# Transposing the 128-row tiles of x1 as pairs of 64-row halves, with the two waits of a tile's transposes made into one per pair

## The chip, the cores and the metric

The kernel runs on one NeuronCore of a Trainium2 chip. The time is device time in microseconds of one execution; the median of three runs is given. The engines are TensorE (PE in the profile; its weight loads are PEld), VectorE (DVE), ScalarE (ACT), GpSimd (POOL), and SyncE (SP), which here only issues DMAs.

## The reference, cut to what matters

The input x is 8 x 32 x 512 x 512 in f32 (268 MB). Two layers:

```python
x = x + conv3x3_int8(group_norm(x), weight, bias)   # layer 0; its result is called x1
x = x + irfft2(R * rfft2(group_norm(x))[low modes]) # layer 1: 32 x 16 modes, mixing channels
```

Layer 0 normalises, quantises to integers with one scale for the whole tensor, and convolves. Layer 1 needs only 16 frequencies along the width and 32 along the height, so its forward transform is made as small matrix products.

## The kernel before, in words

Three stages follow each other.

1. Statistics of x: 128 groups of 2 MB are read and summed (up to about 660 us).
2. The middle stage (about 660 to 2290 us), which the change touches. It works on 256 tiles `t`, 32 for each of the 8 images. A tile is 32 channels x 16 image rows x 512 columns, 1 MB, laid out as 128 partitions (4 rows x 32 channels) by 4 groups `g` of 512. A ring `ring` of XS = 9 slots holds the tiles.
3. The mixing of modes (about 2290 to 2330 us) and then the inverse transform, added to x1 and stored (to the end).

In the middle stage one loop over `i` is written out on every engine, and each engine runs its instructions in the written order:

- SP loads tile t with four DMAs of 256 KB (L242). It may load into a slot once the tile that was there has been stored, transposed and squared.
- ACT scales one half of tile i+1 (`scaled`, L337); DVE scales the other half and makes the quantised image and a shifted copy (L557 to L575).
- PE convolves tile i-2: 48 bf16 matmuls of 32 weight columns and 512 moving columns (`conv`, L732), four of them side by side in four column strips of the array.
- DVE adds the convolution to x in the slot, in two halves (`combine`, L580): the slot now holds x1. GpSimd stores it with four DMAs (L296).
- PE transposes tile i-4 (`turn_x1`, L743): 4 column blocks `v` x 4 groups `g`, each a 128x128 f32 transpose. The data are the weights that are loaded, and the identity `id_s` is the moving operand. Block v goes to PSUM bank 4 + v % 2; v = 0 and 1 come before the convolution, v = 2 and 3 after it. Semaphore `s_t` counts one per block.
- ACT copies each bank to `xt` (`turned`, L345, counted by `s_te`) and squares the tile in between (`squared`, L352).
- PE multiplies the transposed tile i-5 with 32 columns of cosines and sines (`along_w1`, L753).
- The small steps of an image run in the tiles of the next image: `turn_rows` (L770), `along_h1` (L777), `combos` (L784) and a few others.

The transposes are ordered by these waits: block v waits until the copy of block v - 2 is done, so two copies may be under way while PE goes on, and `along_w1` waits for all four copies of its tile.

Of the kernel before, what the change touches and what calls it, by code (L numbers as in the profile page):

```python
# [9 lines left out]
ACT = mybir.ActivationFunctionType  # L10
# [4 lines left out]
HW = 512  # L15
# [12 lines left out]
def build(nc, x, wt, bias, rt, eh, ew, gj, ei, ident, mean, gsel, bsel, comb, gsum, gbc, pavg, negm, out):  # L28
# [5 lines left out]
    T = B * NCH  # L34
    SL = 8
    XS = 9
# [14 lines left out]
    with ctx:  # L51
        def sb(name, shape, dt=F32):
            return ctx.enter_context(nc.sbuf_tensor(name, shape, dt))

        def sem(name):
            return ctx.enter_context(nc.semaphore(name))
# [13 lines left out]
        id_s = sb("id_s", [128, 128])  # L70
# [26 lines left out]
        def bank(k, p=128):  # L97
            return ps[k // 4][0:p, (k % 4) * 512:(k % 4 + 1) * 512]
# [12 lines left out]
        xt = area[:, 2 * qn + FC:2 * qn + 3 * FC].rearrange("p (s v f) -> p s v f", s=2, v=4)  # L111
# [13 lines left out]
        def xslot(k):  # L125
            return ring[:, k * FC:(k + 1) * FC]
# [3 lines left out]
        def gslot(k):  # L130
            return ring[:, k * FT:(k + 1) * FT] if k < 4 else (vbuf, mixb, x2)[k - 4][:, 0:FT]
# [9 lines left out]
        def eslot(k):  # L141
            return xslot(k)
# [41 lines left out]
        s_t = sem("x1_transposed")  # L184
        s_te = sem("x1_transposed_copied")
# [37 lines left out]
        @block.sync  # L223
        def _(sp):
            for dst, src in ((eh_s[:], eh), (ew_s[:], ew), (gj_stage, gj), (ei_s[:], ei), (id_s[:], ident), (mean_s[:], mean),
                             (gsel_s[:], gsel), (bsel_s[:], bsel), (comb_s[:], comb),
                             (gsum_s[:], gsum), (gbc_s[:], gbc), (pavg_s[:], pavg), (negm_s[:], negm)):
                sp.dma_start(dst, src).then_inc(s_const, 16)

            for n in range(NT):  # L230

                if n >= NGS:
                    sp.wait_ge(s_sq, n - NGS + 1)
                for c in range(GC):
                    sp.dma_start(gslot(n % NGS)[:, c * FC:(c + 1) * FC],
                                 x_chan[GC * n + c]).then_inc(s_g_in[n % NGS], 16)


            def load(t):
                b, m = divmod(t, TB)  # L240
                for r in range(4):
                    sp.dma_start(xslot(t % XS)[32 * r:32 * r + 32, :].rearrange("p (g w) -> p g w", g=4),  # L242
                                 x_rows[b, m, r]).then_inc(s_x_in[t % XS], 16)

            for t in range(XS):
                if t < 8 and t % 2 == 0:
                    sp.wait_ge(s_sq, max(n for n in range(NT) if n % NGS == t // 2) + 1)
                load(t)
            for t in range(1, T - XS + 1):
                sp.wait_ge(s_x_out[(t - 1) % XS], ((t - 1) // XS + 1) * 64)  # L250
                sp.wait_ge(s_t, 4 * t)
                sp.wait_ge(s_ss, t)
                load(t + XS - 1)

            for k in range(4, 8):
                sp.wait_ge(s_x_out[k], len(range(k, T, XS)) * 64)
            last = max(t for t in range(T) if 4 <= t % XS < 8)
            sp.wait_ge(s_t, 4 * (last + 1))
            sp.wait_ge(s_ss, last + 1)
            sp.dma_start(ring[:, 4 * FC:8 * FC], rt).then_inc(s_rl, 16)  # L260
            for k in (0, 1, 2, 3, 8):
                sp.wait_ge(s_x_out[k], len(range(k, T, XS)) * 64)
            sp.wait_ge(s_t, 4 * T)
            sp.wait_ge(s_ss, T)

            for k in range(SL):
                if k == 4:
                    sp.wait_ge(s_mx, 4)
                sp.dma_start(eslot(k), x1_chan[k]).then_inc(s_e_in[k], 16)
            with sp.Fori(1, GT // SL) as i:  # L270
                for k in range(SL):

                    sp.wait_ge(s_e_out[k], i * 16)
                    sp.dma_start(eslot(k), x1_chan[ds(i * SL + k, 1)].rearrange("o p f -> (o p) f")).then_inc(
                        s_e_in[k], 16)
            for k in range(SL):
                sp.wait_ge(s_e_out[k], (GT // SL) * 16)
# [30 lines left out]
        def _(act):  # L308
# [23 lines left out]
            def scaled(t):  # L332
                b = t // TB
                act.wait_ge(s_x_in[t % XS], (t // XS + 1) * 64)
                if t >= 2:
                    act.wait_ge(s_r, t - 1)
                act.activation(u[:, t % 2, 0:HF], xslot(t % XS)[:, 0:HF], ACT.Identity,  # L337
                               bias=qtab[:, 2 * B + b:2 * B + b + 1],
                               scale=qtab[:, B + b:B + b + 1]).then_inc(s_ua, 1)

            def turned(t, v):
                act.wait_ge(s_t, 4 * t + v + 1)
                if t >= 2 and v == 0:
                    act.wait_ge(s_w, t - 1)
                act.activation(xt[:, t % 2, v], bank(4 + v % 2), ACT.Copy).then_inc(s_te, 1)  # L345

            def squared(t):
                b, m = divmod(t, TB)
# [6 lines left out]
            def w_copied(t):  # L355
                b, m = divmod(t, TB)
                act.wait_ge(s_w, t + 1)
                if b and m == 3:
                    act.wait_ge(s_vt, 8 * b)
                act.activation(vbuf[:, (m - 3) * 128:(m + 1) * 128], bank(6), ACT.Copy).then_inc(s_ve, 1)  # L360
# [18 lines left out]
            for i in range(T + 20):  # L379
                b, j = divmod(i - (TB + 5), TB)  # L380
                small = i >= TB + 5
                if i + 1 < T:
                    scaled(i + 1)
                if 6 <= i and i - 6 < T and (i - 6) % 4 == 3:
                    w_copied(i - 6)
                if small and j == 6:
                    h_copied(b)
                if small and 1 <= j < 5:
                    rows_copied(b, 2 * j - 1)
                if 4 <= i and i - 4 < T:  # L390
                    turned(i - 4, 0)
                    turned(i - 4, 1)
                    squared(i - 4)
                if small and j < 4:
                    rows_copied(b, 2 * j)
                if 4 <= i and i - 4 < T:
                    turned(i - 4, 2)
                    turned(i - 4, 3)
                if small and j == 12:
                    root(b)  # L400

# [56 lines left out]
            for k in range(SL):  # L458
                t = GT - SL + k
# [223 lines left out]
        def _(pe):  # L683
# [25 lines left out]
            for n in range(3):  # L709
                last = nc.tensor.transpose(bank(0, NT)[:, 128 * n:128 * n + 128],  # L710
                                           stat[:, (n + 1) * NT:(n + 2) * NT], id_s[:])
# [25 lines left out]
            def turn_x1(t, v):  # L737
                if v == 0:
                    pe.wait_ge(s_ev, 2 * t + 2)
                if 4 * t + v >= 2:  # L740
                    pe.wait_ge(s_te, 4 * t + v - 1)
                for g in range(4):
                    last = nc.tensor.transpose(bank(4 + v % 2)[:, 128 * g:128 * g + 128],  # L743
                                               xslot(t % XS)[:, g * HW + 128 * v:g * HW + 128 * v + 128], id_s[:])
                last.then_inc(s_t, 1)

            def along_w1(t):
                pe.wait_ge(s_te, 4 * t + 4)
                if t >= 4 and t % 4 == 0:
                    pe.wait_ge(s_ve, t // 4)  # L750
                for v in range(4):
                    for g in range(4):
                        last = mm(ps[1][32 * g:32 * g + 32, 1024 + 128 * (t % 4):1024 + 128 * (t % 4) + 128],  # L753
                                  ew_s[:, 32 * v:32 * v + 32], xt[:, t % 2, v, 128 * g:128 * g + 128],
                                  start=(v == 0), stop=(v == 3))
                last.then_inc(s_w, 1)

            def turn_rows(b, n):
                if n == 0:
                    pe.wait_ge(s_ve, (b + 1) * TB // 4)  # L760
                    if b:
                        pe.wait_ge(s_x2e, b)
                elif b < B - 1:
                    pe.wait_ge(s_vte, 8 * b + n)
                elif n == 1:
                    pe.wait_ge(s_te, 4 * T)
                else:
                    pe.wait_ge(s_vte, 8 * b + n - 1)
                for c in range(4):
                    last = nc.tensor.transpose(rows_bank(b, n)[:, 128 * c:128 * c + 128], vrows[:, 4 * n + c], id_s[:])  # L770
                last.then_inc(s_vt, 1)
# [198 lines left out]
```

## Time and profile before

| | |
|---|---|
| median of 3 runs | 3610.84 us (3604.45 to 3612.75) |
| the profiled execution | 3599.9 us |
| its span, first to last instruction | 3598.1 us |
| PE busy | 3060.9 us (85%) |
| DVE busy | 3091.9 us (86%) |
| ACT busy | 2371.9 us (66%) |
| transposes of x1 (L743), matmul records | 4096, 559.6 us |
| granted TensorE clock, mean | 0.925 of full speed |

A matmul's record reaches from its start to the end of its latency, and matmuls overlap, so a busy share of PE tells that it has work, and the time between starts tells how fast it works. A share of the span is a mean over stages with different limits; the stage that the change touches has to be read by itself.

### The profile page before, as it was taken

The numbers are of one execution on the slowest core, as the hardware profiler recorded it, in microseconds if no ns is written. First come the engines' busy times: TensorE is split into PE (matmuls) and PEld (weight loads), VectorE is DVE, ScalarE is ACT, GpSimd is POOL, SyncE is SP. The second block draws the span as 40 slices with busy tenths as digits, with TensorE's granted clock in tenths as the row PEclk, the third lists the DMA queues.
The fourth block names the chain that finished last, engine by engine and source line by source line (L and its number), as shares of the span: only waits on it lengthen the run. The fifth ranks groups of instructions, "written<-read, shape, count | busy, mean of one in ns | idle before, by whom it ended". The sixth has DMA issues, their size and how long they took to land.

```text
span 3598.1 us, 81875 instructions
## 1 busy us (share of the span) xinstructions
PE 3060.9 (85%) x33273; PEld 1524.8 (42%) x33273; DVE 3091.9 (86%) x3288; ACT 2371.9 (66%) x3523; POOL 695.4 (19%) x1040
## 2 busy tenths in 40 slices
PE   5666666599999999999999999688888888888886
PEld 1111111266666666666666666433222222222222
DVE  6999999998898989898898989399888888888887
ACT  6888888689898888889898988433333333333332
POOL 0000000144344444444443444000000000000000
PEclk7777777799999999999999999799999999999998
DMA  9999999899999999999999999499999999999998
GB/s 398 421 422 421 421 421 421 271 362 362 308 351 341 347 331 344 344 346 356 317 366 312 356 335 327 159 384 427 427 427 427 427 427 427 427 427 427 427 423 370
DMA packets 342542, 1352.57 MB, mean 376 GB/s; under 512 B 45792, under 2 KB 47040, under 8 KB 243808
## 3 DMA queue, kind: packets, MB, share of 16 engines
q1 hardware_dynamic: 223104, 811.13, 60.0%
q0 software_dynamic: 82272, 268.58, 20.4%
q10 hardware_dynamic: 36864, 268.45, 17.7%
q8 instruction: 237, 3.88, 0.5%
q14 instruction: 65, 0.53, 0.0%
HBM read 811.10 MB, written 536.87 MB: 375 GB/s over the span
## 4 chain that ended last, share of the span: by engine, by line
PE 44%; DMA 41%; DVE 6%; ACT 4%; issue 3%; SPq 1%; DVEq 0%; ACTq 0%
DMA out<-ring 20%; PE ps L732 18%; PE ps L743 13%; DMA ring<-x_scratch 9%; DMA ring<-in_x 8%; PE ps L753 7%; DMA x<-in_x 3%; ACT area L320 3%; DVE ring L669 3%; PE ps L694 2%; DMA mixb<-in_x 1%; DVE stat L485 1%; PE ps L770 1%; PE ps L777 1%; DMA vbuf<-in_x 1%
## 5 line engine op out<-in xcount | busy, mean ns | idle before, releaser
L296 POOL DMA_DIRECT2D x_scratch<-ring x1024 | 689.4, 680 | 1565.1 <-DVE ring L580 1543.3
L884 PE MATMUL ps<-x,gj_s 128*128 128x512 bf16 x3072 | 772.8, 405 | 210.7 <-DVE ring L669 209.7
L580 DVE SCALAR_TENSOR_TENSOR ring<-ps,sc,ring 128x1024 f32<-128x1024 f32 x512 | 650.5, 1282 | 158.1 <-PE ps L732 151.3
L669 DVE TENSOR_TENSOR ring<-ps,ring 128x1024 f32<-128x1024 f32 x512 | 603.0, 1219 | 157.5 <-DMA ring<-x_scratch 154.6
L732 PE MATMUL ps<-area,wq 128*32 128x512 bf16 x12264 | 716.8, 381 | 13.7 <-DVE area L575 8.7
L345 ACT ACTIVATE area<-ps 128x512 f32<-128x512 f32 x1024 | 556.2, 599 | 182.5 <-PE ps L743 176.3
L884 PEld LDWEIGHTS ps<-x,gj_s 128*128 128x128 bf16 x3072 | 294.4, 102 | 766.8 <-DVE ring L669 438.5
L485 DVE TENSOR_REDUCE stat<-area 128x1 f32<-128x4096 f32 x128 | 565.3, 4416 | 45.1 <-ACT area L320 44.2
L743 PE MATMUL ps<-id_s,ring 128*128 128x128 f32 x4096 | 559.6, 280 | 6.5 <-ACT area L345 4.2
L352 ACT ACTIVATE area<-ring,qtab 128x2048 bf16<-128x2048 f32 x256 | 517.0, 2019 | 0.0
L743 PEld LDWEIGHTS ps<-id_s,ring 128*128 128x128 f32 x4096 | 441.5, 141 | 162.1 <-issue 153.6
L437 ACT ACTIVATE x<-ps 128x512 bf16<-128x512 f32 x256 | 152.8, 597 | 522.2 <-PE ps L873 522.1
L732 PEld LDWEIGHTS ps<-area,wq 128*32 128x32 bf16 x12264 | 304.0, 96 | 341.9 <-issue 49.1
L337 ACT ACTIVATE area<-ring,qtab 128x1024 int16<-128x1024 f32 x256 | 317.8, 1242 | 26.7 <-DMA ring<-in_x 10.9
L694 PE MATMUL ps<-ring,negm_s 128*32 128x512 f32 x1184 | 209.8, 844 | 130.0 <-DMA ring<-in_x 130.0
L430 ACT ACTIVATE mixb<-area 32x64 f32 (+1 forms) x512 | 102.5, 247 | 298.4 <-DVE ring L669 294.9
L873 PE MATMUL ps<-ei_s,mixb 32*128 32x512 f32 x512 | 287.7, 642 | 2.2 <-ACT mixb L430 2.2
L753 PE MATMUL ps<-area,ew_s 128*32 128x128 f32 x8192 | 277.1, 276 | 1.5 <-ACT area L345 1.3
L320 ACT ACTIVATE area<-ring,stat 128x4096 f32<-128x4096 f32 x74 | 274.5, 3709 | 2.4
L753 PEld LDWEIGHTS ps<-area,ew_s 128*32 128x32 f32 x8192 | 208.1, 109 | 44.9 <-issue 43.3
L557 DVE TENSOR_SCALAR area<-ring,qtab 128x1024 int16<-128x1024 f32 x256 | 205.9, 804 | 0.1
L656 DVE TENSOR_TENSOR x<-ps,x 64x512 f32<-64x512 f32 x256 | 177.8, 695 | 13.9 <-ACT x L437 4.2
(137 smaller groups left out, 2187.3 us busy)
## 6 DMA issues: line engine op xcount, KB each, us to landing
ring<-in_x SPq DMA_DIRECT2D x1024, 256.0 KB, 7.4
x_scratch<-ring POOLq DMA_DIRECT2D x1024, 256.0 KB, 6.7
ring<-x_scratch SPq DMA_DIRECT2D x256, 1024.0 KB, 11.0
out<-ring ACTq DMA_DIRECT2D x256, 1024.0 KB, 25.8
ring<-in_x SPq DMA_DIRECT2D x148, 1024.0 KB, 20.3
vbuf<-in_x SPq DMA_DIRECT2D x36, 1024.0 KB, 21.0
mixb<-in_x SPq DMA_DIRECT2D x36, 1024.0 KB, 21.1
x<-in_x SPq DMA_DIRECT2D x36, 1024.0 KB, 21.1
```

The lines of the kernel that those rows point to most:

```text
L296: pool.dma_start(x1_rows[b, m, r], xslot(t % XS)[32 * r:32 * r + 32, :].rearrange("p (g w) -> p g w", g=4)).then_inc(s_x_out[t % XS], 16)
L320: act.activation(sqs[:, n % 2], gslot(n % NGS), ACT.Square, bias=st(1, n), accum_out=st(2, n)).then_inc(s_sq, 1)
L337: act.activation(u[:, t % 2, 0:HF], xslot(t % XS)[:, 0:HF], ACT.Identity, bias=qtab[:, 2 * B + b:2 * B + b + 1], scale=qtab[:, B + b:B + b ...
L345: act.activation(xt[:, t % 2, v], bank(4 + v % 2), ACT.Copy).then_inc(s_te, 1)
L352: act.activation(junk_q, xslot(t % XS), ACT.Square, bias=qtab[:, 3 * B + b:3 * B + b + 1], accum_out=ssq[:, (b % 2) * TB + m:(b % 2) * TB ...
L485: nc.vector.tensor_reduce(st(3, n), sqs[:, n % 2], AXX, ALU.max).then_inc(s_max, 1)
L580: nc.vector.scalar_tensor_tensor(out=half, in0=ps[0][:, h * HF:(h + 1) * HF], scalar=col(26), in1=half, op0=ALU.mult, op1=ALU.add).then_in ...
L669: nc.vector.tensor_tensor(half, ps[0][:, hj * 2 * HW:(hj + 1) * 2 * HW], half, ALU.add).then_inc(s_add, 1)
L732: last = mm(ps[0][32 * cg:32 * cg + 32, HW * g:HW * g + HW], wq[:, (3 * a + dw) * C:(3 * a + dw + 1) * C], src[:, 1 + dw:1 + dw + HW], sta ...
L743: last = nc.tensor.transpose(bank(4 + v % 2)[:, 128 * g:128 * g + 128], xslot(t % XS)[:, g * HW + 128 * v:g * HW + 128 * v + 128], id_s[:])
L753: last = mm(ps[1][32 * g:32 * g + 32, 1024 + 128 * (t % 4):1024 + 128 * (t % 4) + 128], ew_s[:, 32 * v:32 * v + 32], xt[:, t % 2, v, 128 * ...
L884: last = mm(bank(j), gj_s[:, (j * 3 + v) * 128:(j * 3 + v + 1) * 128], (z12, z12, z13)[v][:, k % 2], start=(v == 0), stop=(v == 2))
```

## The change

Each 128x128 transpose becomes two: rows 0 to 63 of the tile against a 64x64 identity, and rows 64 to 127 against another, with k = 0 into bank 4 and k = 1 into bank 5. Each loads 64 rows x 128 columns as weights and moves 64 columns. They use the upper and the lower half of the array's rows. Both banks are filled by one pair of blocks (v = 0, 1 or v = 2, 3), so `s_t` now counts once per pair, and ACT copies two banks after that one wait, still 128 x 512 each, but with an output in runs of 64 elements. `s_te` counts once per pair too. The waits of SP and of the later PE steps are only renumbered.

```diff
             def turn_x1(t, v):
                 if v == 0:
                     pe.wait_ge(s_ev, 2 * t + 2)
-                if 4 * t + v >= 2:
-                    pe.wait_ge(s_te, 4 * t + v - 1)
+                if t or v:
+                    pe.wait_ge(s_te, 2 * t + v // 2)
                 for g in range(4):
-                    last = nc.tensor.transpose(bank(4 + v % 2)[:, 128 * g:128 * g + 128],
-                                               xslot(t % XS)[:, g * HW + 128 * v:g * HW + 128 * v + 128], id_s[:])
-                last.then_inc(s_t, 1)
+                    for k in range(2):
+                        c0 = 256 * (v % 2) + 64 * g
+                        last = nc.tensor.transpose(bank(4 + k)[:, c0:c0 + 64],
+                                                   xslot(t % XS)[64 * k:64 * k + 64,
+                                                                 g * HW + 128 * v:g * HW + 128 * v + 128],
+                                                   id_s[64 * k:64 * k + 64, 64 * k:64 * k + 64])
+                if v % 2:
+                    last.then_inc(s_t, 1)
...
-            def turned(t, v):
-                act.wait_ge(s_t, 4 * t + v + 1)
-                if t >= 2 and v == 0:
+            def turned(t, pair):
+                act.wait_ge(s_t, 2 * t + pair + 1)
+                if t >= 2 and pair == 0:
                     act.wait_ge(s_w, t - 1)
-                act.activation(xt[:, t % 2, v], bank(4 + v % 2), ACT.Copy).then_inc(s_te, 1)
+                for k in range(2):
+                    last = act.activation(
+                        xt[:, t % 2, 2 * pair:2 * pair + 2].rearrange("p v (g k m) -> p k (v g) m", g=4, k=2)[:, k],
+                        bank(4 + k).rearrange("p (s m) -> p s m", m=64), ACT.Copy)
+                last.then_inc(s_te, 1)
```

The order on PE in one step of the loop without small work, from the transposes of v = 0, 1 to those of v = 2, 3 and the product along the width, is this before (`x1_transposed_copied` is `s_te`, `x1_half_done` is `s_ev`):

```order
L743 MATMUL ps<-id_s,ring 128x128 [waits x1_transposed_copied,x1_half_done]
L743 MATMUL ps<-id_s,ring 128x128 x3
L743 MATMUL ps<-id_s,ring 128x128 [waits x1_transposed_copied]
L743 MATMUL ps<-id_s,ring 128x128 x3
L732 MATMUL ps<-area,wq 32x512 [waits x1_half_done,quantised_done]
L732 MATMUL ps<-area,wq 32x512 x23
L732 MATMUL ps<-area,wq 32x512 [waits x1_half_done]
L732 MATMUL ps<-area,wq 32x512 x23
L743 MATMUL ps<-id_s,ring 128x128 [waits x1_transposed_copied]
L743 MATMUL ps<-id_s,ring 128x128 x3
L743 MATMUL ps<-id_s,ring 128x128 [waits x1_transposed_copied]
L743 MATMUL ps<-id_s,ring 128x128 x3
```

And this in the changed kernel, at the same place:

```order
L747 MATMUL ps<-id_s,ring 128x64 [waits x1_transposed_copied,x1_half_done]
L747 MATMUL ps<-id_s,ring 128x64 x7
L747 MATMUL ps<-id_s,ring 128x64 [waits x1_transposed_copied]
L747 MATMUL ps<-id_s,ring 128x64 x7
L734 MATMUL ps<-area,wq 32x512 [waits x1_half_done,quantised_done]
L734 MATMUL ps<-area,wq 32x512 x23
L734 MATMUL ps<-area,wq 32x512 [waits x1_half_done]
L734 MATMUL ps<-area,wq 32x512 x23
L747 MATMUL ps<-id_s,ring 128x64 [waits x1_transposed_copied]
L747 MATMUL ps<-id_s,ring 128x64 x7
L747 MATMUL ps<-id_s,ring 128x64 [waits x1_transposed_copied]
L747 MATMUL ps<-id_s,ring 128x64 x7
```

Nothing changed places; each run of 8 transposes became one of 16, the names L743, L732 and L753 of before are L747, L734 and L760 now, and the first wait of each run now covers both banks.

ACT's rows for one step are these before (`w_transform_done` is `s_w`, `chunk_landed1` the landing of a load):

```order
L345 ACTIVATE area<-ps 128x512 [waits w_transform_done,x1_transposed]
L345 ACTIVATE area<-ps 128x512 [waits x1_transposed]
L352 ACTIVATE area,ssq<-ring,qtab 128x2048 [waits x1_half_done]
L345 ACTIVATE area<-ps 128x512 [waits x1_transposed] x2
L337 ACTIVATE area<-ring,qtab 128x1024 [waits rounded_done,chunk_landed1]
```

And these in the changed kernel:

```order
L346 ACTIVATE area<-ps 128x8x64 [waits w_transform_done,x1_transposed]
L346 ACTIVATE area<-ps 128x8x64
L356 ACTIVATE area,ssq<-ring,qtab 128x2048 [waits x1_half_done]
L346 ACTIVATE area<-ps 128x8x64 [waits x1_transposed]
L346 ACTIVATE area<-ps 128x8x64
L337 ACTIVATE area<-ring,qtab 128x1024 [waits rounded_done,chunk_landed2]
```

The order and the number of ACT's instructions stay; the second copy of a pair no longer has a wait of its own, and the first one's wait is for both blocks of the pair.

## Rows read from the trace of the kernel before

**Rows 1.** The page: PE's busy tenths and granted clock, 40 slices of 90 us.

```profile
PE   5666666599999999999999999688888888888886
PEclk7777777799999999999999999799999999999998
```

**Rows 2.** Windows of the middle stage: start:end, length, busy us by engine, clock, DMA, GB/s.

```profile
735.00:880.00 145.00, 142.40 (x2370) 91.16 (x2366) 133.13 (x156) 130.22 (x179) 65.86 (x98) 1.00 1.04 365
1190.00:2190.00 1000.00, 990.29 (x16494) 642.23 (x16486) 885.42 (x1094) 880.12 (x1225) 436.64 (x648) 1.00 1.01 341
```

**Rows 3.** The same windows, L337 alone (one per tile): busy (x count), clock, DMA, GB/s.

```profile
735.00:880.00 145.00, 29.82 (x24) 1.00 1.04 365
1190.00:2190.00 1000.00, 200.24 (x162) 1.00 1.01 341
```

**Rows 4.** The timeline of one plain tile: start, us, engine, line, count, idle before.

```profile
1003.18 2.78 PE L732 MATMUL ps<-area,wq 128*32 128x512 bf16 x48
...
1005.83 2.48 DVE L580 SCALAR_TENSOR_TENSOR ring<-ps,sc,ring 128x1024 f32<-128x1024 f32 x2
1005.90 0.86 PEld L743 LDWEIGHTS ps<-id_s,ring 128*128 128x128 f32 x8 [0.42 <-issue]
1005.90 1.09 PE L743 MATMUL ps<-id_s,ring 128*128 128x128 f32 x8
1006.59 1.09 ACT L345 ACTIVATE area<-ps 128x512 f32<-128x512 f32 x2 [0.61 <-PE ps L743]
1006.92 0.81 PEld L753 LDWEIGHTS ps<-area,ew_s 128*32 128x32 f32 x32 [0.17 <-issue]
1006.92 1.08 PE L753 MATMUL ps<-area,ew_s 128*32 128x128 f32 x32
...
1007.93 1.09 PE L743 MATMUL ps<-id_s,ring 128*128 128x128 f32 x8
...
1008.96 2.78 PE L732 MATMUL ps<-area,wq 128*32 128x512 bf16 x48
...
1011.22 1.28 DVE L580 SCALAR_TENSOR_TENSOR ring<-ps,sc,ring 128x1024 f32<-128x1024 f32 x1
```

**Rows 5.** Weight loads and matmuls by line, whole program: duration ns min/median/max.

```profile
L753 PEld LDWEIGHTS ps<-area,ew_s x8192: 106/110/111, 703.4 to 2269.3; 128*32 128x32 f32 x200
L753 PE MATMUL ps<-area,ew_s x8192: 272/273/298, 703.4 to 2269.4; 128*32 128x128 f32 x200
L777 PEld LDWEIGHTS ps<-mixb,eh_s x128: 132/137/137, 922.1 to 2279.1; 128*64 128x64 f32 x128
L777 PE MATMUL ps<-mixb,eh_s x128: 592/592/643, 922.1 to 2279.5; 128*64 128x512 f32 x128
L796 PEld LDWEIGHTS ps<-dc,pavg_s x16: 192/192/192, 955.1 to 2282.1; 128*128 128x128 f32 x16
L873 PEld LDWEIGHTS ps<-ei_s,mixb x512: 181/184/284, 2331.8 to 3573.0; 32*128 32x128 f32 x171
```

**Rows 6.** The same view of the transposes, from 800 to 2200 us.

```profile
L743 PEld LDWEIGHTS ps<-id_s,ring x3604: 137/140/230, 801.9 to 2200.0; 128*128 128x128 f32 x190
L743 PE MATMUL ps<-id_s,ring x3603: 272/273/476, 801.9 to 2200.0; 128*128 128x128 f32 x190
```

**Rows 7.** Timeline: runs of 32-column products, full rows (L784), half rows (L839).

```profile
1568.15 2.22 PE L784 MATMUL ps<-comb_s,dbuf 128*32 128x32 f32 x128
...
2291.16 1.45 PE L839 MATMUL ps<-x,ring 64*32 64x16 f32 x128 [1.95 <-issue]
```

**Rows 8.** ACT's copies by their output's form, 800 to 2200 us.

```profile
L364 ACT ACTIVATE mixb<-ps 128x512 f32<-128x512 f32 x56 | 34.2, 611 | 0.0
L360 ACT ACTIVATE vbuf<-ps 128x512 f32<-128x512 f32 x56 | 33.3, 594 | 0.0
```

**Rows 9.** Waits from 735 to 900 us: who waited for whom, us, times, longest.

```profile
ACT area L337 <- DMA ring<-in_x: 10.9, 11, 2.1
ACT area L345 <- PE ps L743: 6.6, 11, 0.7
```

More of the change, by code:

```diff
@@ L250, in _ @@
                 sp.wait_ge(s_x_out[(t - 1) % XS], ((t - 1) // XS + 1) * 64)
-                sp.wait_ge(s_t, 4 * t)
+                sp.wait_ge(s_t, 2 * t)
                 sp.wait_ge(s_ss, t)
@@ L257, in _ @@
             last = max(t for t in range(T) if 4 <= t % XS < 8)
-            sp.wait_ge(s_t, 4 * (last + 1))
+            sp.wait_ge(s_t, 2 * (last + 1))
             sp.wait_ge(s_ss, last + 1)
@@ L262, in _ @@
                 sp.wait_ge(s_x_out[k], len(range(k, T, XS)) * 64)
-            sp.wait_ge(s_t, 4 * T)
+            sp.wait_ge(s_t, 2 * T)
             sp.wait_ge(s_ss, T)
@@ L391, in _ @@
                     turned(i - 4, 0)
-                    turned(i - 4, 1)
                     squared(i - 4)
@@ L396, in _ @@
                 if 4 <= i and i - 4 < T:
-                    turned(i - 4, 2)
-                    turned(i - 4, 3)
+                    turned(i - 4, 1)
                 if small and j == 12:
@@ L739, in turn_x1 @@
                     pe.wait_ge(s_ev, 2 * t + 2)
-                if 4 * t + v >= 2:
-                    pe.wait_ge(s_te, 4 * t + v - 1)
+                if t or v:
+                    pe.wait_ge(s_te, 2 * t + v // 2)
                 for g in range(4):
-                    last = nc.tensor.transpose(bank(4 + v % 2)[:, 128 * g:128 * g + 128],
-                                               xslot(t % XS)[:, g * HW + 128 * v:g * HW + 128 * v + 128], id_s[:])
-                last.then_inc(s_t, 1)
+                    for k in range(2):
[6 more added lines that the diff above has]
+                    last.then_inc(s_t, 1)
             def along_w1(t):
-                pe.wait_ge(s_te, 4 * t + 4)
+                pe.wait_ge(s_te, 2 * t + 2)
                 if t >= 4 and t % 4 == 0:
@@ L765, in turn_rows @@
                 elif n == 1:
-                    pe.wait_ge(s_te, 4 * T)
+                    pe.wait_ge(s_te, 2 * T)
                 else:
```

## Prediction

> **What bounds the kernel now.** I read the page's slices first. PE's busy tenths stand at 9 from the ninth slice to the twenty-fifth, and nowhere else, and the granted clock is at 9 there too [rows 1]: the middle stage is where PE works without a break, and that stage is the only one that the change touches. Then the windows of that stage. From 1190 to 2190 us PE is busy 990 of 1000 us at clock 1.00, that is the level of 2.4 GHz; DVE is busy 885 and ACT 880, and the DMA engines show 1.01 with 341 GB/s [rows 2]. PE sets the pace there. L337 runs once per tile, so its count gives the pace: 162 in 1000 us, 6.17 us per tile [rows 3].
>
> The timeline of one plain tile says where PE's time goes. By the starts, the convolution takes 1003.18 to 1005.90 = 2.72 us, a run of 8 transposes 1.02, the product along the width 1.01, the second run 1.03: 5.78 us [rows 4]. The remaining 0.39 us of the 6.17 are the small steps of an image, averaged over its 32 tiles. DVE, when it is behind, needs 1005.83 to 1011.22 = 5.39 us [rows 4], and by its busy time 885/162 = 5.47 us; ACT needs 880/162 = 5.43 us [rows 2, 3]. So both are only 0.7 us per tile behind PE.
>
> The third look is at DMA, and it is the one that decides most here. A tile moves 2.10 MB (1 MB in, 1 MB out). From 735 to 880 us, where no small step runs yet, PE alone would keep 5.78 us per tile. But there were 24 tiles in 145 us, 6.04 us each [rows 3], and ACT waited 11 times for a load [rows 9]. The transfers were late there with the DMA engines at 1.04. The bytes of that window are 365 GB/s [rows 2], which is 5.75 us per tile: 25.2 tiles' bytes moved while 24 tiles were used, since some engines' loads ran ahead of the slowest. So the pace that DMA alone allows lies between 5.75 and 6.04 us per tile.
>
> **The change, part by part.**
>
> *The pace of a transpose.* A run's time is 8 pitches and a switch: 1.02 us to the next step's start, with 0.17 us idle on the load side just before it [rows 4], so 0.85/8 = 0.106 us per transpose. Two things could be that pitch. The moving side: f32 matmuls of 512 and 128 columns last 592 and 273 ns [rows 5, 6], 0.83 ns per column, so 128 columns take 106 ns over a fixed 167. The load side: plain f32 loads of 32 and 64 columns last 110 and 137 ns, and of 128 columns 192 [rows 5], 0.84 ns per column over a fixed 84 or so; the transposing load of 128 columns lasts only 140 [rows 6], some 55 ns over it. So the moving identity is the bound, and the load has half its time.
>
> *The new pair.* 16 transposes stand where 8 did. Each moves 64 columns (64 x 0.83 = 53 ns) and loads 128 columns (again some 55 ns, if the load does not care for rows: 32 rows take 184 ns where 128 take 192 [rows 5]). If the two halves of the array work beside each other, a pair takes about 55 ns; if one after another, 106 to 112, which is what it takes now. No row shows two 64x128 parts at once. The nearest are the 32-column products: with all 128 rows, 128 records take 2.22 us, 17.3 ns each; with 64 rows in two halves, and 16 moving columns in place of 32, 1.45 us, 11.3 ns each [rows 7]. A round over four column strips costs 4 x 17.3 = 69 ns, a round over eight parts 8 x 11.3 = 91 ns. With the same columns to load, the second half of the rows adds a third to the round and doesn't double it. I take "beside each other", and keep the other end for the rivals. Then a run is 8 x 0.055 + 0.17 = 0.61 us, and two runs save 2 x 0.42 = 0.84 us per tile of PE.
>
> By the Trainium skill ("TensorE: Matmul & The Clock Gate", section on LDWEIGHTS) a load takes its columns over 1.2 GHz whatever its rows. That would be 107 ns for each of these loads; the row of 140 ns against 192 speaks against it for a transposing load, and it is the rule under the rival "loads one by one" below.
>
> *The new wait.* Before, the copies of a run's banks start 0.69 us after the run and end 1006.59 + 1.09 = 1.78 us after it; the next run starts 2.03 us after it [rows 4]: 0.25 us to spare. Now both copies wait for the whole run. The last pair starts at about 0.39 us, ends 0.22 later (its own 53 ns and the fixed 167), plus the 0.10 us that ACT takes to start, so the copies run from 0.71 to 1.80 us. PE, now faster, would come to the next run at 0.61 + 1.01 = 1.62 us, and waits some 0.2 us. The other run has the convolution (2.72 us) between it and the next, and 1.1 us of copies fit. In the four tiles of an image with `turn_rows` that step covers the wait. Behind the waiting transpose stand the convolution and then `combine`, but DVE is not starved, since PE's plain tile is now 5.78 - 0.84 + 0.2 = 5.14 us, or 5.53 with the small steps. Without the gain of the pair the same wait is 1.12 + 1.09 against 2.03: 0.2 us on the path.
>
> *The copies.* Output in 64-element runs: a copy into a split form takes 611 ns, into a plain one 594 [rows 8]. Four of them add at most 0.07 us to ACT's 5.43 per tile. Taken as hidden; it costs the whole only if ACT is the bound.
>
> *The sum.* PE needs 5.53, DVE 5.47, ACT 5.50, DMA 5.75 to 6.04 us per tile. DMA ends last. I take 6.0, near the upper end, because there the rate is counted by tiles that were used, in a stretch where loads were late; the lower end counts bytes that ran ahead, and they cannot run ahead for ever in a ring of nine. So 6.17 - 6.0 = 0.17 us on some 250 tiles: 43 us. Of the 160 to 210 us that PE gives up, three quarters go to the wait for loads. The profiled execution of 3599.9 us would take 3557; the median of the runs shown is 10.9 us above it, so 3567.
>
> **The rivals.**
>
> - *DMA allows 5.75.* All engines then pace at about 5.75, and 0.42 x 250 = 105 us go: 3506. For it: the bytes of rows 2. Against it: 11 waits at 6.04. Between the two, gains of 25 to 105 us are one case with a moving size.
> - *DMA already is the pace.* If stores and loads at 6.1 to 6.2 us per tile are all that it can do, the gain is under 7 us: 3605 to 3611. For it: 1.01 share over 1000 us at 6.17. Against it: the stretch in which loads were late went at 6.04, and a share of 1.04 [rows 2, 3], so 6.17 at 1.01 is not the limit.
> - *The pair is not side by side.* PE keeps its 5.78 and gets the wait of 0.2 us: 5.98 in 28 of 32 tiles, and 0.39 on top, some 6.34. That is 0.17 x 250 = 43 us slower: 3654. It decides from the point where a pair takes more than 0.095 us, since then the 0.2 of the wait is not paid for. For it: the load has no slack in a pair. Against it: the rounds of rows 7.
> - *Loads one by one, at 0.106 us.* 16 loads make a run 1.87 us, 0.85 more than now, twice per tile, and the wait of 0.25: 8.1 us per tile, 480 us slower: 4090. For it: 192 ns for a plain f32 load of 128 columns. Against it: 140 ns for the transposing one. The rule of the Trainium skill on LDWEIGHTS named above would give this time if loads of different rows cannot overlap; its part on packing small matmuls says that they can.
> - *ACT becomes the bound*, through the split output: it would have to lose 0.5 us per tile, seven times what rows 8 allow. Not priced further.
>
> **How the numbers follow.** This kernel's runs can tell a difference of about 0.2%, 7 us. Pair side by side with a gain of 25 to 75 us: 0.45; the same with more, up to 115 us: 0.17; DMA already the pace: 0.13; not side by side: 0.14; loads one by one, or something between it and the last: 0.11. That gives faster 0.62, same 0.13, slower 0.25. The likeliest case by itself runs from 3535 to 3590. The range must reach from the second case, 3510, to the fourth, 3660; what is above it and the far end of the second are left out.
>
> **What would show each step.** Right: starts of the first and last load of a run 0.4 us apart, not 0.75; the next step 0.6 us after the run's start; waits of PE for L346 of about 0.2 us per tile; ACT waiting for loads over the whole stage and not just at its start; L337 counted 166 or 167 times in 1000 us; PE's busy share under 0.95 with the clock still at 1.00. Wrong: a pair of 0.107 us or more in the run (the third or fourth rival), or no wait for loads although the pace is below 5.9 (the first).

## The result and the profile after

| | before | after |
|---|---|---|
| median of 3 runs | 3610.84 us | 3645.99 us (3641.95 to 3655.85) |
| ratio | | 1.0106, 95% interval 1.0077 to 1.0135 |
| profiled span | 3598.1 us | 3640.1 us |
| PE busy | 3060.9 us | 2932.9 us |
| PE and PEld records | 33273 each | 37369 each |

The change is slower by 1.1%, though PE has 128 us less to do. The page of the changed kernel, the slices that answer to [rows 1], and the groups of the transposes:

```profile
PE   5666666589889898898899898688887888888886
PEclk8777787799999999999999999899999999999998
...
L747 PE MATMUL ps<-id_s,ring 64*128 64x64 f32 x8192 | 374.0, 230 | 73.5 <-ACT area L346 56.6
L747 PEld LDWEIGHTS ps<-id_s,ring 64*128 64x128 f32 x8192 | 305.7, 139 | 242.6 <-issue 175.3
```

PE's nines have turned into eights and nines: it is no longer busy without a break. The windows of the middle stage, which answer to [rows 2], with one row for L337 alone, which answers to [rows 3]:

```profile
735.00:880.00 145.00, 128.51 (x2700) 77.75 (x2696) 129.53 (x153) 127.03 (x176) 65.39 (x98) 0.99 1.03 358
1190.00:2190.00 1000.00, 893.81 (x18586) 555.91 (x18582) 863.58 (x1071) 860.90 (x1196) 426.21 (x632) 0.98 0.99 333
...
1190.00:2190.00 1000.00, 197.03 (x158) 0.98 0.99 333
```

158 tiles in 1000 us where there were 162. PE is idle for 106 of the 1000 us, DVE and ACT are less busy than before as well, and DMA, though its engines are still near full (0.99), moves less (333 GB/s, not 341). So something makes PE wait. Its timeline over four tiles (the plain tile of before is in [rows 4]):

```profile
1052.96 0.71 PE L747 MATMUL ps<-id_s,ring 64*128 64x64 f32 x16
1053.60 1.08 PE L760 MATMUL ps<-area,ew_s 128*32 128x128 f32 x32
1054.94 0.71 PE L747 MATMUL ps<-id_s,ring 64*128 64x64 f32 x16 [0.26 <-ACT area L346]
1055.59 2.78 PE L734 MATMUL ps<-area,wq 128*32 128x512 bf16 x48
1058.30 1.02 PE L747 MATMUL ps<-id_s,ring 64*128 64x64 f32 x16
...
1069.52 0.71 PE L747 MATMUL ps<-id_s,ring 64*128 64x64 f32 x16
1070.16 0.86 PE L760 MATMUL ps<-area,ew_s 128*32 128x128 f32 x22
1073.15 0.69 PE L760 MATMUL ps<-area,ew_s 128*32 128x128 f32 x10 [2.14 <-issue]
1073.78 1.11 PE L747 MATMUL ps<-id_s,ring 64*128 64x64 f32 x16
```

Three things are to be seen. The run of 16 takes 1053.60 - 1052.96 = 0.64 us to the next step, against 1.02 for the 8 of before: the halves do work side by side. The run after the product along the width now starts 1.34 us after that product in place of 1.01. And in the last tile there is a hole of 2.14 us in the middle of 32 equal matmuls, where no semaphore is waited for: after 22 of them PE had nothing to do. The transposes after that hole take 1.11 us where 0.71 is usual, and the window around it shows the granted clock at 0.72, a mean of the two levels:

```profile
1072.00:1078.00 6.00, 4.85 (x66) 2.60 (x70) 2.50 (x4) 3.55 (x5) 2.07 (x3) 0.72 1.05 413
```

PE's waits, from 700 to 2250 us, first of the changed kernel:

```profile
PE ps L747 <- ACT area L346: 50.2, 165, 1.3
PE ps L734 <- issue: 37.7, 39, 3.8
PE ps L760 <- issue: 28.2, 25, 2.9
PE ps L791 <- issue: 17.7, 8, 4.8
PE ps L747 <- issue: 14.4, 18, 4.1
```

and of the kernel before:

```profile
PE ps L784 <- issue: 7.6, 3, 2.6
PE ps L770 <- ACT vbuf L360: 4.5, 7, 2.6
PE ps L732 <- issue: 2.9, 2, 1.7
PE ps L743 <- ACT area L345: 2.4, 4, 0.9
```

Waits for ACT's copies went from 2 to 50 us, and "issue", a wait for nothing that the profile names, from 13 to 98 us.

### The profile page after: what moved, and what is told of

It reads as the page before. It is cut to its first block, busy times and chain, and to the rows that moved or that the text cites. A ratio compares the mean times of both kernels' runs of the same rounds, so it can differ in the third digit from the quotient of the medians.

```text
span 3640.1 us, 90067 instructions
## 1 busy us (share of the span) xinstructions
PE 2932.9 (81%) x37369; PEld 1405.0 (39%) x37369; DVE 3086.5 (85%) x3288; ACT 2370.6 (65%) x3523; POOL 695.3 (19%) x1040
## 4 chain that ended last, share of the span: by engine, by line
DMA 42%; PE 29%; DVE 11%; issue 9%; ACT 9%; SPq 1%; DVEq 0%; POOL 0%; ACTq 0%
DMA out<-ring 20%; PE ps L734 15%; DMA ring<-x_scratch 9%; DMA ring<-in_x 8%; PE ps L747 7%; ACT area L346 3%; ACT area L320 3%; DVE ring L671 3%; DMA x<-in_x 2%; DVE ring L582 2%; PE ps L696 2%; PE ps L760 2%; DMA vbuf<-in_x 1%; DMA mixb<-in_x 1%; ACT area L356 1%
## 5 line engine op out<-in xcount | busy, mean ns | idle before, releaser
L734 PE MATMUL ps<-area,wq 128*32 128x512 bf16 x12264 | 754.3, 389 | 50.4 <-issue 38.1
L734 PEld LDWEIGHTS ps<-area,wq 128*32 128x32 bf16 x12264 | 316.4, 98 | 380.3 <-issue 91.7
L747 PE MATMUL ps<-id_s,ring 64*128 64x64 f32 x8192 | 374.0, 230 | 73.5 <-ACT area L346 56.6
L747 PEld LDWEIGHTS ps<-id_s,ring 64*128 64x128 f32 x8192 | 305.7, 139 | 242.6 <-issue 175.3
L337 ACT ACTIVATE area<-ring,qtab 128x1024 int16<-128x1024 f32 x256 | 319.1, 1247 | 23.3 <-DVE area L564 8.8
L760 PE MATMUL ps<-area,ew_s 128*32 128x128 f32 x8192 | 286.7, 276 | 29.5 <-issue 28.2
L760 PEld LDWEIGHTS ps<-area,ew_s 128*32 128x32 f32 x8192 | 210.7, 109 | 54.6 <-issue 35.7
```

The lines of the kernel that those rows point to most:

```text
L734: last = mm(ps[0][32 * cg:32 * cg + 32, HW * g:HW * g + HW], wq[:, (3 * a + dw) * C:(3 * a + dw + 1) * C], src[:, 1 + dw:1 + dw + HW], sta ...
L747: last = nc.tensor.transpose(bank(4 + k)[:, c0:c0 + 64], xslot(t % XS)[64 * k:64 * k + 64, g * HW + 128 * v:g * HW + 128 * v + 128], id_s[ ...
```

## What the holes are: PE runs out of fetched instructions

The DMA view of both kernels, from 1190 to 2190 us, has a queue that the kernel's text knows nothing of. Before, and after:

```profile
q8 instruction: 130, 2.13, 0.9%
```

```profile
q8 instruction: 146, 2.39, 1.0%
```

Its packets are of 2.13 MB / 130 = 16.4 KB. In the same windows PE and PEld show 16494 + 16486 records before and 18586 + 18582 after, 254 and 255 for each packet. So this queue brings PE its instructions, some 256 at a time. Where DMA is idle, in the mixing stage of the kernel before, the time of such a fetch can be read:

```profile
2285.00:2300.00 15.00, 7.08 (x575) 6.58 (x571) 3.01 (x10) 1.57 (x8) 0.00 (x0) 0.62 0.02 6
...
2294.90 1.43 PE L839 MATMUL ps<-x,ring 64*32 64x16 f32 x128 [2.29 <-issue]
2298.37 0.78 PE L839 MATMUL ps<-x,ring 64*32 64x16 f32 x57 [2.04 <-issue]
```

The window's DMA share is 0.02. PE gets through 128 matmuls with their 128 loads, 256 records, in 1.4 us, and then waits 2.0 to 2.3 us: 3.5 to 3.7 us from block to block (2291.16 of [rows 7], 2294.90, 2298.37). In the middle stage of the changed kernel PE would use up a block in 256/235 of a tile, some 5.8 us. That is longer than 3.7, so on an idle DMA it would not have to wait (an estimate from these rows).

The instructions and packets of the traces show that the holes are such waits. A "gap" below is a hole of over 0.3 us between two weight loads of the same line. Counted over all of PE's instructions, those for semaphores included, the instruction behind a gap is always number 193 modulo 256 (the first is number 0), the same place of a block: so it is for all 100 gaps in the changed kernel's middle stage, for the 7 before, and for all 352 in the 14 traces of this document. And each of them ends 1.1 to 1.7 us after a packet of q8 has landed. So PE stands there because its next block isn't there yet. (The gaps count idle time of the loads; their sum, 129 us, is larger than the 98 us of "issue" on PE's matmuls.) The packet itself does not take longer on full DMA engines: the median is 1.06 us in the changed kernel and 1.07 before, against 0.9 to 1.4 with DMA idle. It starts later. Behind a gap, the next packet starts 4.2 us (median of 100) after PE has gone on, 3.4 in the kernel before (7 gaps), where with DMA idle it is 0.9. With the packet's own 1.1 us and some 1.4 behind it, that makes 6.7 us, more than the 5.8 that a block lasts.

The Trainium skill ("Runtime: NRT & Kernel Launch", section on instruction fetch mechanics) says that instructions come in blocks of 16 KiB, 256 each, over a DMA queue of the engine's own, and that the cost of it is mostly hidden. The trace agrees with the block. That the cost is mostly hidden holds for the kernel before (13 us of "issue") and not for the changed one (98 us).

Two theories came out of this. **F**: fetches come late, because PE asks for instructions faster and the DMA queues are full. **W**: the loss is the common wait of both banks. They don't exclude each other; the question is what each costs.

## The experiments

The middle stage of each, measured between L337 of the tenth and of the last tile in its trace; records per tile are PE and PEld together, and "PE idle for ACT" holds the waits of the small steps too. Each row is one execution, which can lie off the median time: that of e1 is 17 us below it, that of e10 10 us above it.

| | us per tile | records per tile | gaps | PE idle for ACT |
|---|---|---|---|---|
| before | 6.18 | 203 | 14.7 us | 7 us |
| after | 6.34 | 235 | 129.3 us | 67 us |
| e1, after with 32 fewer | 6.05 | 203 | 38.1 us | 96 us |
| e2, before with 32 more | 6.34 | 235 | 42.9 us | 2 us |
| e3, before with the common wait | 6.43 | 203 | 12.2 us | 59 us |
| e4, before with 32 fewer | 6.13 | 171 | 8.5 us | 5 us |
| e5, after, half the stores | 6.14 | 235 | 94.2 us | 62 us |
| e6, before, half the stores | 6.14 | 203 | 12.1 us | 2 us |
| e7, after, second run moved | 6.53 | 235 | 29.6 us | 227 us |
| e8, e7 with bf16 product | 6.59 | 203 | 23.8 us | 347 us |
| e9, after, half the stores and loads | 5.77 | 235 | 6.3 us | 72 us |
| e10, before with bf16 product | 6.07 | 171 | 17.7 us | 89 us |
| e11, pairs in the first run only | 6.21 | 219 | 42.5 us | 52 us |
| e12, e11 with bf16 product | 6.05 | 187 | 24.0 us | 169 us |

**e1: fewer instructions, the same work.** The product along the width is made of half as many matmuls with twice the columns; the modes come out wrong.

```diff
-                for v in range(4):
+                for v in range(2):
                     for g in range(4):
-                        last = mm(ps[1][32 * g:32 * g + 32, 1024 + 128 * (t % 4):1024 + 128 * (t % 4) + 128],
-                                  ew_s[:, 32 * v:32 * v + 32], xt[:, t % 2, v, 128 * g:128 * g + 128],
+                        last = mm(ps[1][32 * g:32 * g + 32, 1024 + 256 * (t % 2):1024 + 256 * (t % 2) + 256],
+                                  ew_s[:, 32 * v:32 * v + 32], xt[:, t % 2, 2 * v + g // 2, 256 * (g % 2):256 * (g % 2) + 256],
```

> The changed kernel with 32 PE instructions fewer per tile and the same columns moved: the product along the width is issued as 8 matmuls of 256 moving columns in place of 16 of 128 (its numbers are wrong and the modes with them; time and traffic are kept). Theory F (PE runs out of fetched instructions while the DMA queues are full): the changed kernel has 101 gaps of over 0.3 us inside a run of equal matmuls, 131 us together, against 16 and 25 us before; with the instruction count of before they fall under 50 us, and the time to between 3560 and 3605 us. Theory W (the new common wait of both banks costs the time): the waits stay, and so does the time, 3640 to 3655 us.

Measured: 3586.98 us, ratio to before 0.9948 (0.9929 to 0.9967). With 32 records fewer the changed kernel is not slower but faster, by some 59 us against itself. The gaps fell from 129 to 38 us while the waits for ACT rose from 67 to 96: F, not W, for this part. Among its waits from 1190 to 2190 us those for loads are twice what they were in the changed kernel (15.5 us against 7.3):

```profile
ACT area L337 <- DMA ring<-in_x: 15.5, 19, 1.6
```

**e2: more instructions, the same work.** The last 16 matmuls of the convolution, cut in two.

```diff
+                            n_w = 2 if dw == 2 else 1
+                            for w0 in range(0, HW, HW // n_w):
...
-                                      wq[:, (3 * a + dw) * C:(3 * a + dw + 1) * C], src[:, 1 + dw:1 + dw + HW],
+                                          src[:, 1 + dw + w0:1 + dw + w0 + HW // n_w],
```

> The kernel before, with 32 PE instructions more per tile and the same columns moved: the last 16 of the 48 matmuls of the convolution are cut into two of 256 columns. Transposes and waits are those of before. Theory F: gaps inside runs of equal matmuls appear as in the changed kernel, over 70 us together where there were 25, and the time rises by 40 to 130 us, to 3650 to 3740. Theory W: nothing is added to any wait, so the time stays within 0.3% of the kernel before (it could rise by 10 us for the cut matmuls' own cost).

Measured: 3639.85 us, 1.0087 (1.0053 to 1.0121). The kernel gets slower by 31 us with 32 more records per tile and the same columns; the cut convolution itself takes 0.02 us longer (2.73 by its starts against 2.71), 5 us of the 31. The gaps rose less than I expected, from 15 to 43 us, and the time a little less than expected too. The same number of records makes 129 us of gaps in the changed kernel: it gets through the rest faster, in 5.34 us of a plain tile in place of 5.78, and so asks for blocks faster.

**e3: the common wait alone.** The changed kernel with 128x128 transposes put back.

```diff
-                    for k in range(2):
-                        c0 = 256 * (v % 2) + 64 * g
...
+                    last = nc.tensor.transpose(bank(4 + v % 2)[:, 128 * g:128 * g + 128],
+                                               xslot(t % XS)[:, g * HW + 128 * v:g * HW + 128 * v + 128], id_s[:])
```

> The waits of the change alone: 128x128 transposes as before, but both banks are filled before ACT copies them, and PE waits for both copies. Theory F: the instruction count is that of before, gaps stay near 25 us, and the time rises only by the wait, at most 0.2 us in 28 of 32 tiles, 0 to 43 us. Theory W: the whole loss of the change and more shows here, 3645 to 3665 us.

Measured: 3672.22 us, 1.0216 (1.0153 to 1.028), over the end of both expectations. The wait alone costs 63 us, more than the whole change. Its timeline:

```profile
1506.45 1.09 PE L744 MATMUL ps<-id_s,ring 128*128 128x128 f32 x8
...
1507.48 1.08 PE L755 MATMUL ps<-area,ew_s 128*32 128x128 f32 x32
1507.59 1.09 ACT L346 ACTIVATE area<-ps 128x512 f32<-128x512 f32 x2 [0.67 <-PE ps L744]
...
1508.79 0.86 PEld L744 LDWEIGHTS ps<-id_s,ring 128*128 128x128 f32 x8 [0.50 <-issue]
```

The copies end at 1508.68, and the next run loads at 1508.79, 2.34 us after the run before, not 2.03. The gaps stay at 12 us. So W is real, it costs more than either theory had, and F adds nothing here.

**e4: the cut of e1 in the kernel before.**

> The kernel before with the same cut as the first run, 32 PE instructions fewer per tile with the same columns moved (numbers of the modes wrong). PE's work of 5.78 us per plain tile stays. Theory F: the 25 us of gaps shrink to under 10, the time falls by 10 to 25 us, since PE's matmuls still set the pace. Theory W: no change, 3600 to 3615 us.

Measured: 3593.35 us, 0.9962 (0.9945 to 0.9979), 15 us faster, gaps 8.5 us: in F's range. The gaps themselves fell by only 6 us; the product's own run got 0.01 to 0.02 us shorter, some 4 us, and the rest is not explained.

**e5 and e6: half the stores of x1 left out, after and before.**

```diff
-                for r in range(4):
+                for r in range(2):
                     pool.dma_start(x1_rows[b, m, r],
```

> The changed kernel with half the stores of x1 left out (two of the four DMAs per tile; the last stage reads x in place of x1, with the same traffic, so its output is not the reference's). PE's instructions and waits are those of the changed kernel. Theory F says that a fetch comes late because it queues behind the tiles' transfers: with 1.57 MB per tile in place of 2.10, DMA is no longer full, the gaps inside runs fall from 129 us to under 40, and the pace of the stage to 5.6 to 5.85 us per tile, 100 us or more below the changed kernel. A rival, G, says that PE's fetch has a rate of its own, whatever the DMA queues carry: the gaps stay near 100 us and the pace over 6.0.

> The same two stores per tile left out of the kernel before (again x read in place of x1 at the end). PE's work of 5.78 us per plain tile sets the pace with or without them. Theory F: pace 6.13 to 6.17 us per tile, at most 15 us faster in all, and slower than the changed kernel with the same cut by 70 us or more. Rival G: the same for this kernel, but then the changed one is not faster than it.

Measured: 3598.84 us, 0.9969 (0.995 to 0.9989) for the changed kernel, and 3590.97 us, 0.9955 (0.9942 to 0.9968) for the other. The expectation of F for e5 failed: the gaps only went to 94 us and the pace to 6.14. So did its expectation for e6: the changed kernel should have been faster than it by 70 us and is 8 us slower, as G has it. The DMA share was still 0.92 in both, so this didn't empty the queues, and the pair of tests doesn't decide between F and G.

**e9: half the stores and half the loads left out.**

```diff
-                for r in range(4):
+                for r in range(4 if t < XS else 2):
                     sp.dma_start(xslot(t % XS)[32 * r:32 * r + 32, :].rearrange("p (g w) -> p g w", g=4),
```

> The changed kernel with half the stores and, from the tenth tile on, half the loads left out too (output not the reference's). Leaving out the stores alone took the gaps inside runs only from 129 to 95 us. F, narrowed: the fetches queue behind the loads and stores together, so with half of both the gaps fall under 40 us and the pace of the stage to 5.9 us per tile or less. G: a fetch of 256 instructions has a time of its own (3.4 to 3.8 us where DMA is idle, by the mixing stage of the kernel before) and bursts on PE run into it: gaps stay at 80 us or more, pace 6.1 to 6.2.

Measured: 3505.75 us, 0.9707 (0.9678 to 0.9736). Its window, from 1190 to 2100 us, and that of the changed kernel:

```profile
1190.00:2100.00 910.00, 857.34 (x18478) 548.75 (x18480) 848.84 (x1059) 847.87 (x1185) 198.84 (x314) 1.00 0.68 183
```

```profile
1190.00:2100.00 910.00, 811.99 (x16960) 504.90 (x16952) 787.91 (x976) 783.15 (x1087) 388.06 (x577) 0.98 0.99 334
```

PE takes more records in the same time, 18478 against 16960, and has next to no gaps: 6 us. G is out: more blocks came in the same time, and on time. Behind the 6 gaps that are left, the next packet of q8 starts after 1.9 us (median), where it is 4.2 in the changed kernel and 3.7 in e5. So a block comes late when the DMA engines are near full (share 0.92 to 1.02 in these runs), and hardly ever at 0.68. The clock is at 1.00 again. The waits for ACT are still there, 72 us.

**e7 and e8: the second run between the halves of the convolution**, with ACT's squares after the second pair of copies; e8 has the product along the width in bf16 as well.

```diff
                     conv(i - 2, 0)
-                    conv(i - 2, 1)
                 if 4 <= i and i - 4 < T:
                     turn_x1(i - 4, 2)
                     turn_x1(i - 4, 3)
+                if 2 <= i and i - 2 < T:
+                    conv(i - 2, 1)
```

> The changed kernel with its second run of transposes put between the two halves of the convolution, and ACT's squares put after the second pair of copies. Both runs then have 1.36 us or more of other PE work behind them. Theory W (part of the loss is the common wait after the second run, 0.3 us per tile by the run with the waits alone): PE's idle time before transposes for ACT falls from 50 us to under 15, one more switch of 0.17 us per tile is added, so PE's tile is 0.15 us shorter. Theory F: PE then asks for instructions still faster, the gaps inside runs stay at 100 us or more, and most of the 0.15 us is lost in them: 3610 to 3645 us. If W were the larger part, it would come to 3590 or lower.

> The split order, and the product along the width in bf16 (ACT writes the transposed tile as bf16, the cosines are rounded to bf16): 16 matmul records per tile in place of 32, 0.4 us in place of 1.0. PE's instructions per tile are again those of the kernel before, and its own work is some 4.7 us of a tile that DMA lets through in 6.0. Theory F: PE has a microsecond per tile to hide late fetches in, PE sets nothing, ACT waits for loads over the whole stage, pace 5.95 to 6.05 us, 3560 to 3585 us. If DMA's limit were the 5.75 of its bytes, 3510.

Measured: 3688.47 us, 1.0226 (1.0205 to 1.0247), and 3698.35 us, 1.0242 (1.0218 to 1.0265). Both expectations are wrong. I had only counted PE's side. The trace of e7:

```profile
1559.90 0.71 PE L747 MATMUL ps<-id_s,ring 64*128 64x64 f32 x16
1560.03 1.24 ACT L337 ACTIVATE area<-ring,qtab 128x1024 int16<-128x1024 f32 x1
...
1561.16 0.59 ACT L364 ACTIVATE vbuf<-ps 128x512 f32<-128x512 f32 x1
...
1561.64 0.60 ACT L368 ACTIVATE mixb<-ps 128x512 f32<-128x512 f32 x1
...
1562.12 1.10 ACT L346 ACTIVATE area<-ps 128x512 f32<-128x512 f32 x2
...
1563.27 0.71 PE L747 MATMUL ps<-id_s,ring 64*128 64x64 f32 x16 [1.25 <-ACT area L346]
```

With the squares at the end, ACT is still at them and at L337 when the first run is done, so its copies start 2.2 us after the run's start, where 0.75 is usual. In this tile two small copies (L364, L368) stand in between as well; in one without them (1593.67 to 1595.59) it is still 1.9. The second run stands 1.36 us of convolution behind the first and waits for them. PE waits for ACT 227 and 347 us. In e8 it also stands at the lower clock level for 147 us of the stage, against 27 in e7. The gaps fall with PE's pace, to 30 and 24 us. What makes these two so slow is what ACT is at when the first run is done, on top of the common wait that e3 priced.

**e10: the kernel before with the product along the width in bf16.** ACT writes `xt` as bf16, the cosines are rounded once; one record of a matmul in place of two.

```diff
-                                  ew_s[:, 32 * v:32 * v + 32], xt[:, t % 2, v, 128 * g:128 * g + 128],
+                                  ewb_s[:, 32 * v:32 * v + 32], xt[:, t % 2, v, 128 * g:128 * g + 128],
```

> The kernel before (128x128 transposes, a wait per bank) with the product along the width in bf16: 32 PE instructions fewer per tile and 0.6 us less of PE's time, so PE needs 5.2 us of a plain tile without any common wait. If fetches and waits are what the changed kernel lost by, this is DMA's pace undisturbed: gaps under 15 us, 5.95 to 6.05 us per tile, 3560 to 3590 us. If something else held the changed kernel at over 6.0 (ACT's or DVE's share), it stays above 3600.

Measured: 3566.86 us, 0.9869 (0.9831 to 0.9907). Here the loads are late over the whole stage; from 1190 to 2190 us:

```profile
ACT area L338 <- DMA ring<-in_x: 37.3, 34, 2.9
```

The pace is 6.07 us per tile at 348 GB/s, where the changed kernel was expected to be. The gaps (18 us) and the pace came out just above the expectation, the time within it. SyncE's waits for stores of x1 rose too, from 9 us in the kernel before to 114. So this is near what DMA allows. That DMA alone sets it isn't shown: ACT waits longer for PE (68 us) than for loads.

**e11 and e12: pairs only in the first run of a tile**, where the convolution hides the common wait; e12 with the bf16 product too.

```diff
+                if t or v >= 2:
+                    pe.wait_ge(s_te, 3 * t + v // 2)
                 for g in range(4):
+                    if v < 2:
+                        for k in range(2):
```

> 64-row pairs in the first run of a tile only, where the convolution hides the common wait; the second run is as before, with a wait per bank. PE saves 0.42 us per tile, gets 16 instructions more, and no wait of 0.3 us. Theory W: PE's idle time for ACT's copies goes from 50 us to under 10. Theory F: gaps of 30 to 60 us. Together 5.95 to 6.1 us per tile, 3575 to 3610 us.

> The two of these together: pairs in the first run, the product along the width in bf16. PE's work is 4.75 us per plain tile with fewer instructions than before. If DMA sets the pace, as the run with bf16 alone should show, the pairs bring nothing on top: within 0.3% of it, 3560 to 3590 us. If PE still mattered, it would be 20 us or more below.

Measured: e11 3602.45 us, 0.9984 (0.9968 to 1.0), a gain of at most 0.3%. The gaps are 42 us, as F has it, and the waits for ACT 52, where W had under 10. Against the kernel before that is 28 and 45 us more, some 70 of the 90 us that the pairs save on PE (0.38 x 246); ACT waits 29 us of the 1000 for loads as well. e12 3562.82 us, 0.9858 (0.9829 to 0.9888). That is the fastest with full traffic, and not apart from e10: with 0.4 us less on PE per tile nothing is gained, so PE doesn't set the pace in either.

## Why the prediction was wrong

The time lies in the range, and the sign is wrong. By its steps:

- *The pace of a transpose, and the new pair*: right. The two halves of a pair start 4 to 5 ns apart, in loads and in matmuls, and pairs follow each other at 0.062 us where 0.055 was worked out. A run takes 0.64 us where 0.61 was, so the two runs save 0.76 us per tile, not 0.84. The load's 140 ns was laid to its transposing; but L770, also an f32 transpose of 128x128, from a source with a stride, loads in 193 ns (median of 256 in the kernel before), so 140 holds for this source only. The rivals "not side by side" and "loads one by one" are out. That the time lies in the range at all is owed to the first of them, which the range had to reach. It gave 3654 us, and that this is near the 3646 measured is chance: its own price was a pair of 0.106 us, which did not come.
- *The new wait*: the mechanism was right and the term was too small. I let the next run start as the copies end, at 1.80 us. It starts 1054.94 - 1052.96 = 1.98 us after the run before: ACT starts at 0.75, the copies end at 1.84, and PE takes another 0.1 us and more to start. So PE waits 0.33 us, not 0.2. By e3, such a wait costs 63 us where it stands alone.
- *The copies*: right, 603 ns where 599 was.
- *The sum* is the step that failed, where it says "PE needs 5.53 [...] DMA ends last". PE's need was summed from its matmuls and one wait. Two things were missing. Instructions are a supply too: 203 records per tile became 235, and PE would go through them faster, while the queue that brings them shares 16 full DMA engines. The sum put that at nothing. It made 129 us of gaps where there were 15, and the clock fell to 0.98 behind them. Taking the 32 records away again gives 59 us back (e1), adding them to the kernel before costs 31 (e2), halving the traffic takes the gaps away (e9). The second is the size of the wait.
- *DMA's own pace of 6.0*: near, as far as the runs show. e1, e10 and e12, with fewer records than the changed kernel, run at 6.05 to 6.07 with loads late, and no run with full traffic came near 5.75. The changed kernel never got there.
- *DMA already the pace*, the second rival: its pace of 6.1 to 6.2 gives up to 17 us (0.07 x 250), not under 7. It plays no part in what happened.
- *The rival that ended slower* needed a pair that isn't side by side. The real one, a supply of instructions, was not among them, though its parts were in the trace: the q8 rows, and the waits of 2 us for "issue" in the stage of rows 7, one row of which the prediction used for another purpose.

The runs' differences don't add up, since each part hides behind the others. Along PE alone an estimate comes near. A plain tile went from 5.78 to 5.34 us with the wait of 0.33 in it: 246 x 0.44 = 108 us less. The gaps are 115 us more. PE stood at the lower clock level for 61 us of the stage, 7 before, which at half the pace is at most 27 us more. Together that is 7 to 34 us slower; the stage, by its pace, got 38 us slower (246 x 0.156). What the clock costs was not separated by a run.

## What to carry to other kernels

Where a change makes more and smaller instructions, count the records per unit of work and look for "issue" holes inside runs of equal instructions: in this unrolled program PE's instructions were fetched by the same DMA engines that carry its data. With PE and DMA both near full, 32 records saved per tile gave 59 us in the changed kernel and 15 in the one before, with the same columns moved. And a wait that covers two buffers cost 0.31 us per tile (e3) where 1.0 us of other work stood between the two runs, and nothing where the convolution's 2.7 us did. So it belongs behind long work on the engine that waits, and the engine that copies must be free when it is posted (e7).

## What the runs showed of the hardware

- A block of 256 PE instructions took 3.5 to 3.7 us to come with DMA idle, and for 235 records per 5.3 us of work it came late 100 times in 246 tiles with the DMA share at 0.99, but 6 times at 0.68. Its packet took 1.1 us in both; it was the packet's start that came later.
- All 352 gaps of over 0.3 us inside a line's weight loads, in 14 traces, stand at the same place of a block of 256 PE instructions, and end 1.1 to 1.7 us after a packet of q8 landed.
- Two 64x128 f32 transposes in the two halves of the array's rows, to two PSUM banks, followed each other at 0.062 us per pair, where 128x128 ones do at 0.109 (medians of the starts, 800 to 2200 us).
- A hole of 2.1 us on PE was followed by matmuls at the lower clock: 0.72 granted over the 6 us around it.
